# The score mask written into PSUM by ScalarE, one output projection per eight heads, and the values right behind the scores, in a windowed-attention stack of six layers

## What is computed

```python
qkv = x @ Wqkv                       # 128 -> 3 x 16 heads x 64
q = l2norm(q) * qs;  k = l2norm(k) * ksc      # then rotary tables
# windows of 32 queries look at 64 keys: their own window and the one before
mask = (it < jb) | (it > jb + w) | (jb == -1)
sim = where(mask, -max, einsum('bhwie,bhwje->bhwij', bq, bk2) * 8)
out = einsum('bhwij,bhwje->bhwie', softmax(sim), bv2)
x = out @ Wo + x
xn = layernorm(x) * g + bln
a, gate = split(xn @ W1 + b1, 2)     # 2 x 341 columns
x = a * gelu(gate) @ W2 + b2 + x
```

## Time and profile before

| what | value |
|---|---|
| median of 3 runs | 2355.35 us (2354.97 to 2357.37) |
| profiled execution, own time | 2357.62 us |
| its span | 2355.8 us |
| PE busy | 2190.8 us (93%) |
| PE weight loads | 1570.5 us (67%) |
| VectorE busy | 1528.4 us (65%) |
| ScalarE busy | 1652.2 us (70%) |
| GpSimd busy | 1365.7 us (58%) |
| mean granted TensorE clock | 0.975 |

### The profile page before, as it was taken

How to read it: one execution, slowest core, us unless ns; L and a number is a source line. 1 busy time by engine, 2 the same in 40 slices (tenths; PEclk the granted TensorE clock), 3 DMA queues, 4 the chain that set the end, 5 groups by cost and what they waited for, 6 DMA issues and landing times.

```text
span 2355.8 us, 68304 instructions
## 1 busy us (share of the span) xinstructions
PE 2190.8 (93%) x23408; PEld 1570.5 (67%) x23408; DVE 1528.4 (65%) x3440; ACT 1652.2 (70%) x4136; POOL 1365.7 (58%) x1543
## 2 busy tenths in 40 slices
PE   4799999999999999999999999999999688969999
PEld 2466666666666666666666666666666456649998
DVE  6677777777777777777777777777776366651111
ACT  2577878777787777877778787787877455534444
POOL 2787777777777777777777777777776121110000
PEclk7899999999999999999999999999999799979999
DMA  2222232222322223222232222322222200000000
GB/s 78 57 65 59 48 89 59 59 59 47 90 59 59 58 47 91 58 60 57 47 91 57 61 56 48 92 56 62 55 48 63 75 2 1 0 1 3 4 4 7
DMA packets 156776, 119.83 MB, mean 51 GB/s; under 512 B 45806, under 2 KB 148660, under 8 KB 156596
## 3 DMA queue, kind: packets, MB, share of 16 engines
q1 hardware_dynamic: 156724, 119.15, 21.2%
HBM read 23.61 MB, written 1.05 MB: 10 GB/s over the span
## 4 chain that ended last, share of the span: by engine, by line
PE 80%; ACT 10%; issue 4%; DVE 2%; POOL 2%; POOLq 0%; ACTq 0%; DVEq 0%
PE bank L559 8%; PE bank L576 8%; PE bank L543 7%; PE bank L594 7%; PE bank L460 5%; PE bank L505 5%; PE bank L507 5%; PE bank L1391 5%; PE bank L1382 5%; PE bank L479 4%; PE bank L529 4%; PE bank L519 3%; ACT pr L654 3%; PE bank L469 3%; PE bank L488 3%
## 5 line engine op out<-in xcount | busy, mean ns | idle before, releaser
L704 DVE TENSOR_TENSOR t<-bank,rot_t 128x512 f32<-128x512 f32 x384 | 265.5, 691 | 191.3 <-PE bank L505 127.6
L654 ACT ACTIVATE pr<-bank,mx 128x64 f32<-128x64 f32 x1536 | 336.0, 330 | 24.4 <-DVE mx L733 20.7
L793 POOL TENSOR_TENSOR qr<-t 128x512 f32<-128x512 f32 x192 | 244.8, 1275 | 134.8 <-DVE t L705 128.6
L787 POOL TENSOR_TENSOR qr<-qr,rn 128x512 f32<-128x512 f32 x192 | 199.7, 1040 | 192.9 <-DVE rn L687 192.9
L705 DVE TENSOR_TENSOR t<-bank,rot_t 128x512 f32<-128x512 f32 x384 | 261.1, 680 | 0.0
L644 ACT ACTIVATE qT<-bank 128x512 f32<-128x512 f32 x192 | 114.7, 597 | 201.0 <-PE bank L479 201.0
L796 POOL TENSOR_TENSOR sqh<-sq 128x512 f32<-128x512 f32 x192 | 244.7, 1274 | 0.5 <-ACT sq L614 0.5
L799 POOL TENSOR_TENSOR kr<-t 128x512 f32<-128x512 f32 x192 | 244.6, 1274 | 0.0
L559 PEld LDWEIGHTS bank<-kBD,qT 128*32 128x32 f32 x6144 | 156.0, 109 | 121.2 <-issue 121.2
L647 ACT ACTIVATE kBD<-bank 64x512 f32<-64x512 f32 x384 | 224.7, 585 | 3.1 <-PE bank L488 0.8
L594 PE MATMUL bank<-attT,wo 128*128 128x128 f32 x1536 | 217.5, 285 | 0.0
(11 more groups left out here) (171 smaller groups left out, 4573.3 us busy)
## 6 DMA issues: line engine op xcount, KB each, us to landing
vBD<-vS SPq DMA_DIRECT2D x1152, 64.0 KB, 2.0
vBD<-vS SPq DMA_DIRECT2D x576, 32.0 KB, 1.8
wqkv<-in_L_ffn_Wqkv_dram SPq DMA_DIRECT2D x12, 768.0 KB, 6.4
wo<-in_L_ffn_Wo_dram SPq DMA_DIRECT2D x12, 256.0 KB, 2.8
vBD<-in_L_ffn_W_dram SPq DMA_DIRECT2D x1, 2048.0 KB, 9.7
w<-in_L_ffn_W_dram SPq DMA_DIRECT2D x6, 341.0 KB
const<-in_const_dram SPq DMA_DIRECT2D x1, 1478.0 KB, 6.5
out_dram<-acc SPq DMA_DIRECT2D x8, 128.0 KB, 1.8
```

The costliest lines, as they stand in the source:

```text
L654: ins = act.activation(pr[:, slot % 2, hd, :], bank[5][:, hd * 64:(hd + 1) * 64], ACT.Exp, bias=mx[:, slot % 2, hd:hd + 1])
L704: dve.tensor_tensor(t1[:, m], src, tab[:, 0, :].unsqueeze(1).broadcast_to([P, HH, DH]), ALU.mult)
L787: pool.tensor_tensor(x, x, rn[:, slot, half * HH:(half + 1) * HH].unsqueeze(2).broadcast_to([P, HH, DH]), ALU.mult).then_inc(norm.sem, 1)
L793: pool.tensor_tensor(qr[:, slot].rearrange("p (h d) -> p h d", d=DH), t1[:, 0], t2[:, 0], ALU.add).then_inc(q_add.sem, 1)
```

## The change

It has four parts, all in the six layers.

1. The mask. The bf16 matmul L555 goes. ScalarE writes the mask as fp32 from the constants into bank 5 (`seed`, one ACTIVATE of 128x512 per unit), as the first thing in its steps 1 to 4, and once ahead of the loop; the score matmuls add to it. One matmul ahead of the loop writes the whole bank once. Bank 5 no longer serves the up projection: its third chunk goes to bank 6, and so is issued behind the values of step 4 and waits for `pt_ev`. Two bf16 copies of constants in the preparation go.
2. The output projection. Instead of four times 128 tokens it runs twice an iteration over 256 tokens (unit's slot odd: at step 3 for the first eight heads and at step 0 for the others), and VectorE's addition to `uT` likewise.
3. TensorE's order: values right behind the scores, then the third up chunk, the turns of q and k, at step 0 the down projection, then the output projection.
4. ScalarE's order: `seed` first; `ln_scale` ahead of the squares; `xnF` behind the v copy; the exps ahead of the `qT` and `kBD` copies. VectorE's addition L712 goes behind the maximum and L738.

```diff
-        up = (bank[0], bank[1], bank[5])
+        up = (bank[0], bank[1], bank[6])
...
             if c == 2:
-                pe.wait_ge(p_exp.sem, p_exp.after(UPB * (i - 1) + UPB - 1) if live(1) else p_exp.after(UPB * NI - 1))
+                pe.wait_ge(pt_ev.sem, pt_ev.after(UPB * (i - 1) + UPB - 1) if live(1) else pt_ev.after(UPB * NI - 1))
...
         def layers_pe(pe):
+            pe.matmul(bank[5][:, :], ident, cst("rot"), start=True, stop=True).then_inc(s_set.sem, 1)
...
-                if j == 0 and live(3):
-                    down_pe(pe, i, live)
...
                 if j == UPB and live(2):
-                    for c in range(FC):
+                    for c in range(2):
                         up_pe(pe, i, live, c)
+                if j == UPB - 1 and live(2):
+                    pe.wait_ge(qt_ev.sem, qt_ev.after(UPB * (i - 1) + UPB - 1) if live(1) else qt_ev.after(UPB * NI - 1))
+                    ln_turn_out(pe, i - 2, bank[3][:, 0:SEQ])
                 if has(F_S):
...
-                    pe.wait_ge(p_exp.sem, p_exp.after(n - 1))
-                    if j == 0 and live(3):
-                        pe.wait_ge(h_mul.sem, h_mul.after(i - 3))
-                    pe.matmul(bank[5][:, :], bandsel[:, t, :], bandrhs[:, :], start=True, stop=False, skip_group_check=True)
+                    pe.wait_ge(s_seed.sem, s_seed.after(n))
...
-                if has(F_T) and j < UPB:
-                    turn_qk(pe, i, j, live, has, unit)
...
                     mm.then_inc(o_mm.sem, 1)
-                if has(F_O):
+                if j == UPB and live(2):
+                    up_pe(pe, i, live, 2)
+                if has(F_T) and j < UPB:
+                    turn_qk(pe, i, j, live, has, unit)
+                if j == 0 and live(3):
+                    down_pe(pe, i, live)
+                if has(F_O) and unit(F_O)[1] % NT == NT - 1:
...
                     for c in range(HP):
-                        mm = pe.matmul(bank[2][:, 0:P], wo[:, h * HP + c, :], attT[:, h * HP + c, t * P:(t + 1) * P],
+                        mm = pe.matmul(bank[2][:, 0:SEQ], wo[:, h * HP + c, :], attT[:, h * HP + c, :],
                                        start=(c == 0), stop=(c == HP - 1))
...
         def layers_act(act):
+            def seed(t):
+                act.activation(bank[5][:, :].rearrange("p (h k) -> p h k", h=HH),
+                               band[:, t, :].unsqueeze(1).broadcast_to([P, HH, 2 * WIN]), ACT.Copy).then_inc(s_seed.sem, 1)
+
+            act.wait_ge(s_set.sem, 1)
+            seed(0)
             for i, j, live, has, unit in units(act):
+                if j and live(1):
+                    act.wait_ge(p_exp.sem, p_exp.after(UPB * (i - 1) + j - 1))
+                    seed(j % NT)
                 if j == UPB and live(2):
                     act.preload_act_table(ACT.Gelu)
+                if j == UPB - 1 and live(2):
+                    ln_scale(act, i - 2)
...
                     act.preload_act_table(ACT.Exp)
+                if has(F_S):
+                    _, slot, n = unit(F_S)
+                    act.wait_ge(s_max.sem, s_max.after(n))
+                    for hd in range(HH):
+                        ins = act.activation(pr[:, slot % 2, hd, :], bank[5][:, hd * 64:(hd + 1) * 64], ACT.Exp,
+                                             bias=mx[:, slot % 2, hd:hd + 1])
+                    ins.then_inc(p_exp.sem, 1)
                 if has(F_T):
...
-                if has(F_S):
-                    _, slot, n = unit(F_S)
-                    act.wait_ge(s_max.sem, s_max.after(n))
...
-                    dve.tensor_tensor(u, u, bank[2][:, 0:P], ALU.add).then_inc(u_res.sem, 1)
+                    dve.tensor_tensor(u, u, bank[2][:, 0:SEQ], ALU.add).then_inc(u_res.sem, 1)
...
-            pool.tensor_copy(bandrhs[:, :], cst("band")).then_inc(cast_done.sem, 1)
-            pool.tensor_copy(bandsel[:, :, :], cst("bandsel").rearrange("p (t q) -> p t q", t=NT)).then_inc(cast_done.sem, 1)
```

More of the change, by code:

```diff
@@ L631, in layers_act @@
                 if j == UPB - 1 and live(2):
-                    ln_scale(act, i - 2)
+                    m = i - 2
+                    act.wait_ge(ld_up.sem, ld_up.after(m >> 3))
+                    act.wait_ge(ln_t2.sem, ln_t2.after(m))
+                    act.activation(xnF[:, :], bank[3][:, 0:SEQ], ACT.Identity, bias=lngb[:, 1:2],
+                                   scale=lngb[:, 0:1]).then_inc(ln_out.sem, 1)
                 if j == UPB and live(2):
@@ L707, in layers_dve @@
                                           ALU.mult).then_inc(mul.sem, 1)
[L708 to L713, removed]
                 if has(F_P):
@@ L738, in layers_dve @@
                     dve.tensor_reduce(ss[:, slot, :], sqh[:, :, :], AX.X, ALU.add).then_inc(ss_red.sem, 1)
+                if j == 0 and live(3):
+                    m = i - 3
+                    u = uT[:, seq_cols(m & 7)]
+                    dve.wait_ge(f_mm.sem, f_mm.after(m))
+                    dve.scalar_tensor_tensor(out=u, in0=bank[6][:, 0:SEQ], scalar=b2c[:, 0:1], in1=u,
+                                             op0=ALU.add, op1=ALU.add).then_inc(f_res.sem, 1)
                 if has(F_P):
@@ L745, in layers_dve @@
                                       rinv[:, par, :].unsqueeze(2).broadcast_to([P, HH, DH]), ALU.mult).then_inc(o_norm.sem, 1)
[L746 to L749, removed]
+                if has(F_O) and unit(F_O)[1] % NT == NT - 1:
+                    it, slot, _ = unit(F_O)
+                    n = 2 * it + slot // NT
+                    u = uT[:, seq_cols(it & 7)]
+                    dve.wait_ge(u_res.sem, u_res.after(n - 1))
                     dve.wait_ge(y_mm.sem, y_mm.after(n))
-                    dve.tensor_tensor(u, u, bank[2][:, 0:P], ALU.add).then_inc(u_res.sem, 1)
+                    dve.tensor_tensor(u, u, bank[2][:, 0:SEQ], ALU.add).then_inc(u_res.sem, 1)
         def turn_tables(pool, i):
@@ L768, in layers_pool @@
                     m = i - 2
-                    pool.wait_ge(u_res.sem, u_res.after(UPB * m + UPB - 1))
+                    pool.wait_ge(u_res.sem, u_res.after(2 * m + 1))
                     pool.wait_ge(ln_t1.sem, ln_t1.after(m - 1))
@@ L833, in load_wo @@
         def load_wo(sp, layer, h):
-            sp.wait_ge(y_mm.sem, y_mm.after((layer * NB - 1) * UPB + 2 * h + 1))
+            sp.wait_ge(y_mm.sem, y_mm.after((layer * NB - 1) * 2 + h))
             hold(sp)
@@ L1439, in _ @@
             layers_sp(sp)
-            sp.wait_ge(y_mm.sem, y_mm.after(DEPTH * NB * UPB - 1))
+            sp.wait_ge(y_mm.sem, y_mm.after(DEPTH * NB * 2 - 1))
             sp.dma_start(w1e, A["L1_ffn_W1"].rearrange("e p f -> p e f")).then_inc(ld_exp.sem, 16)
@@ L1500, in _ @@
             gru_pe(pe)
-            pe.wait_ge(cast_done.sem, 4)
+            pe.wait_ge(cast_done.sem, 2)
             pe.wait_ge(zeroed_dve.sem, 1)
@@ L1542, in constants @@
     edge = np.where(j < WIN, NEG, 0.0) + 0.0 * i
[L1543 to L1548, removed]
+    both = np.stack([np.concatenate([band + edge] + [band] * (NWT - 1), 0), np.tile(band, (NWT, 1))], 1)
+    put("band", both.astype(f32))
     tri = np.where(rows[None, :] <= rows[:, None], 0.0, NEG)
```

27 lines of the change are left out of this document (10 added, 17 removed).

## The result

The changed kernel takes 2432.73 us (median of 4 runs, 2429.61 to 2438.54), the kernel before in the same session 2355.99 (2354.97 to 2357.37). The ratio is 1.0328, 95% interval 1.0308 to 1.0349: 3.3% slower. The forecast was 2437. Some of the spread of medians seems to come from outside the six layers: in one set of runs the kernel before took 2355 to 2357 us at a mean granted clock of 0.975 to 0.980 and 2366 to 2367 us at 0.970 to 0.973, while from 200 to 1700 us the granted clock is 1.00 in every profile.

A forecast was written before the change was run, and what follows sets the result against it. TensorE bounds the kernel at 36.88 us an iteration; after the change the ring through ScalarE and VectorE would take 38.6. 1.75 us in 47 iterations, 82 us, gives 2440, or 2437 against the median; range 2385 to 2478.

The forecast's parts named there:

- the ring: Loop from k square through VectorE's maximum, exps, copies and seed to the next square; whole iteration 38.6 us against 36.88.
- The mask's price on ScalarE: Four seeds of 128x512 an iteration at 0.50 us each, raising ScalarE's busy time from 29.21 to 31.2 us.
- B: Stretch from k square of step 1 to that of step 2: 7.59 us forecast, 7.21 before.
- C: Stretch from k square of step 2 to that of step 3: 8.80 us forecast, 7.78 before.
- D: Stretch from k square of step 3 to the exps: 3.53 us forecast, 3.71 before.
- E: Stretch from exps of step 3 to the `ob` transposes at step 0: 10.5 us forecast, 10.27 before.
- F: Stretch from the `ob` transposes at step 0 to q's matmul at step 1: 6.27 us forecast, 5.74 before.
- TensorE's need: TensorE's work in one iteration, claimed to fall by 1.65 us to 35.23, from mask and projection.
- rival 1: TensorE stays the bound and time falls with its work, 78 us in all, to 2278; chance 13%.
- The sum: Whole kernel: 1.75 us more in each of 47 iterations, 82 us, giving 2437 against the median.
- signs that it named: In the new profile: period 38.2 to 39.1 us, maximum waits about 1 us, TensorE waiting for k copies and below 90% busy.
- rival 3: More waits: GpSimd's root for `ln_scale` 1 us late, or a lower granted clock as TensorE idles; 2484 us; chance 10%.

The follow-up runs named there:

- e1: Changed kernel with the mask written by a TensorE matmul again and no ScalarE seeds: +18.0 us against the kernel before, ratio 1.0089.
- e2: Changed kernel with the output projection over 128 tokens four times again: +37.0 us against the kernel before, ratio 1.0157.
- e5: Changed kernel with one more 128x512 ScalarE copy, never read, behind each seed of the loop: +153.7 us against the kernel before, ratio 1.0658.
- e4: Changed kernel with q and k turns ahead of values and ScalarE's copies ahead of exps, as before the change: -4.4 us against the kernel before, ratio 0.9990.
- e3: Changed kernel with the third up chunk ahead of the values in step 4: +39.2 us against the kernel before, ratio 1.0173.
- e7: Changed kernel with seeds behind the squares in steps 1 to 3, behind the pT copy in step 4: +34.3 us against the kernel before, ratio 1.0137.
- e10: Changed kernel with both old orders, third chunk first, seeds between squares (step 4: behind pT copy), VectorE's first projection addition behind the root: 2277 us, ratio 0.9662.
- e12: Kernel before with the wide output projection alone, mask by TensorE and all orders as before: +16.2 us against the kernel before, ratio 1.0057.
- e13: As e12, with VectorE's addition of the first projection behind the inverse root at step 4: 2312 us, ratio 0.9816 against the kernel before.
- e8: As e7, with third chunk ahead of values, ln_scale behind the squares, its result's turn behind the scores: +43.8 us against the kernel before, ratio 1.0189.
- e11: As e10, but VectorE's addition of the first projection stays ahead of the root: -29.0 us against the kernel before, ratio 0.9879.

## Why the prediction was right

**The mechanism.** It said that TensorE bounds the kernel before and that the question is whether the ring fits; by its walk it didn't. That the ring sets the changed kernel's time is shown by e1 and e2 (more TensorE work, less time) and by e5 (1.60 us for ScalarE copies whose sum has room in its gaps).

**The mask's price on ScalarE.** Taken as a slot of 0.50; the seed to `ln_scale` is 0.61 with what follows, and in e5 seed to copy is 0.52. Writing PSUM costs here what reading it did: in the changed kernel a seed lasts 0.59 on average, the 512-column activations out of PSUM 0.59 to 0.64. That ScalarE is quicker into PSUM than into SBUF, as the Trainium skill (ScalarE: Activation LUTs, the step-by-step part) has it, agrees with e5, where activations from the same source take 0.59 on average into PSUM and 0.62 into SBUF (160 each); it is too small to matter.

**The ring, B and C.** 0.12 too long in B, 0.03 too short in C. The near hit in C is in part luck: square to exps was 4.14 for 4.23 and the k copies' slots and the q copy's 1.59 for 1.71, the seed's slot 0.61 for 0.50 and `ln_scale`'s 0.90 for 0.77. The parts are shown one at a time: seeds 0.5 each (e1), exps ahead of the copies 0.51 and 1.24 (e4).

**D and E.** D was 0.16 too long: square to sum was 1.83 and not 1.90, the maximum followed the inverse by 0.13 and not 0.20. E was right to 0.01, but what it said behind the sum, that moving the third chunk costs a values' slot, is only half right: undoing it gives 0.56 (e3). Two more limits lie close below, and the prediction saw neither: 0.56 below, TensorE's own order (e3), and 0.35 and 0.26 below, in e1 and e7, the chain through VectorE's root and GpSimd. (The expectation of e10 counts e3 to the latter; e3's trace has no wait of TensorE for GpSimd's k.) It had called VectorE's wide addition hidden, "since neither stands between square and maximum". That is true, and it isn't the whole of what the addition delays: in the changed kernel the table chain hides it, in e12 nothing does. That was a wrong reason with a right price, and so luck.

**F.** 6.41 for 6.27. v's matmul has a slot of 0.95 with no mask behind it where it had 0.86, so the mask's removal frees 0.22 and not 0.31 (e1 has the same 0.22); the transposes of `ob` take 0.49 for 0.44. The wide projection's 0.83 on this path is shown by e2.

**TensorE's need.** The figure of 35.23 for rival 1 was mis-sized: it took the savings off the whole period, the wait of 0.57 for the exps included, which e12 and e13 no longer have, and the mask's four times 0.31 were 0.22 each. 36.88 - 0.57 - 0.41 - 0.88 is 35.02, and e10 ran at 35.12. The two errors partly cancel. The rival was out for its mechanism, and its price was 0.2 us an iteration too modest.

**The sum.** 1.75 us in 47 iterations was forecast; it was 1.60 in 48. The errors of the stretches, -0.12, +0.03, -0.16 and +0.14 for B, C, D and F, partly cancel, and so do the smaller gain and the larger number of iterations. Of the signs that it named, the period lies between 38.2 and 39.1 and ScalarE's waits for the maximum are 1.09 on average; TensorE's waits ahead of the `ob` transposes are shorter than said (0.59, 1.34 and 0.28 for 0.7, 1.6 and 0.7), and it is busy 91% of an iteration, not below 90%. The clock half of rival 3 didn't come: the granted clock is 1.00 in the layers. Its other half, a late `ln_scale`, didn't either: no wait of that kind is in the changed kernel's list.

The Trainium skill (Perfetto Trace Analysis, Identifying the Most-Contended Engine) names the most occupied engine as the one to relieve. TensorE is that in both kernels. By the slots above the change relieves it by some 1.3 us an iteration (mask 0.88, projection 0.41). In the changed kernel that bought nothing, since a ring in which ScalarE is busy 81% and VectorE 68% grew past it; in e10, with the same matmuls, it did. So the page names the right engine here only once the ring fits.

## What to carry to other kernels

When the bound engine is busy 97% and the change takes work off it, walk the chain through the others once round the loop, with each instruction in its order: an operation on a half idle engine is free only where the engine would wait anyway, and costs its full slot between a result and the next thing that the ring waits for (e5). Put evacuations and seeds where that engine waits anyway. Where one fix gives less than its slot, there is another limit just below: look for a new wait of the bound engine (here TensorE's 0.3 us for GpSimd's k, in e1, e7, e8, e11 and e12), walk back from it, and look for an operation in front of the producer that waits for something unrelated. The length of an idle engine's own wait doesn't tell: GpSimd's for the root is at most 4.1 us in the kernel before, where it costs nothing, and at most 3.9 in e11, where the chain costs 1.11. And when the bound engine has waits left, count them: a change can fill them (e13).

## What the runs showed that was not expected

- Removing a bf16 mask matmul of 128x512 ahead of 32 small score matmuls frees 0.22 us, not the 0.31 from start to start: the 128x512 matmul in front of them then has a slot of 0.95 in place of 0.86.
- An addition of 0.42 us on VectorE is worth 1.11 us an iteration by its place (e13 against e12, e10 against e11), through VectorE, GpSimd and TensorE.
- Two more moves on top of e7 (37.58) made an iteration longer (e8, 37.86).
- The wide projection gave 1.01 us an iteration in e13 and not 0.41: TensorE's wait of 0.57 for the exps at step 1 was gone.
